# A bank for each token tile in the values' sums, zeros between the low halves of the probabilities, and two raw places for the output weights

## What is computed

```
h = layernorm(x);  q = h @ wq (32 heads of 128);  k, v = ctx @ wk, ctx @ wv (8 heads of 128, each for 4 heads of q)
q, k = rope(q), rope(k)
attn = softmax(q k^T / sqrt(128) + mask);  o = attn v;  x1 = x + tanh(g_xattn) * (o @ wo)
h1 = layernorm(x1);  logits = h1 @ route_w^T;  e = argmax(logits)
out = x1 + tanh(g_ffn) * (logits[e] * (h1 @ A[e]^T) @ Bw[e]^T)
```

## Time and profile before

| | us |
|---|---|
| median of 3 runs (lowest, highest) | 1171.74 (1171.24, 1173.85) |
| profiled execution | 1174.4 |
| its span, first to last instruction | 1172.3 |
| PE busy | 1125.3 (96%) |
| DVE busy | 927.2 (79%) |
| ACT busy | 632.2 (54%) |
| POOL busy | 564.2 (48%) |
| idle of PE ahead of line 846, for DVE line 1118 | 15.9 |

### The profile page before, as it was taken

The page is one execution under the profiler, slowest core; times in us unless marked ns, Lnnn a source line. Parts: engine busy times, 40 slices in busy tenths (PEclk is TensorE's granted clock), DMA queues, the critical chain, the costliest instruction groups (busy, mean ns, idle before and its releaser), DMA issues.

```text
span 1172.3 us, 17228 instructions
## 1 busy us (share of the span) xinstructions
PE 1125.3 (96%) x5792; PEld 922.9 (79%) x5792; DVE 927.2 (79%) x1413; ACT 632.2 (54%) x1090; POOL 564.2 (48%) x512
## 2 busy tenths in 40 slices
PE   7999999799999999999999999999999999999997
PEld 6788887677777777777778777888888888888775
DVE  7984747888778778787888888788888877788877
ACT  6452355556666666666665444555555555555441
POOL 4651467676666666666653323233333333333320
PEclk9999999899999999999999999999999999999999
DMA  6869963494545454535368625542435342431101
GB/s 225 281 226 371 301 221 129 142 365 140 190 135 189 135 189 135 189 135 190 117 224 339 191 97 157 160 163 90 168 112 188 112 166 91 162 125 65 64 1 72
DMA packets 88902, 197.89 MB, mean 169 GB/s; under 512 B 8304, under 2 KB 41200, under 8 KB 82928
## 3 DMA queue, kind: packets, MB, share of 16 engines
q1 hardware_dynamic: 88816, 196.79, 48.8%
HBM read 113.92 MB, written 82.84 MB: 168 GB/s over the span
## 4 chain that ended last, share of the span: by engine, by line
PE 49%; POOL 17%; DVE 14%; issue 13%; ACT 4%; DMA 1%; DVEq 0%; SPq 0%; POOLq 0%; ACTq 0%
PE attn L846 18%; PE proj L784 12%; POOL rot L1575 6%; PE attn L736 4%; PE score L801 4%; POOL wq_s L1550 3%; PE turned L736 2%; PE score L736 2%; DVE q_r L1033 2%; DVE o_s L1118 2%; DVE p_low L1111 2%; DVE acc L1130 2%; PE turned L812 2%; ACT p_high L1395 1%; PE attn L828 1%
## 5 line engine op out<-in xcount | busy, mean ns | idle before, releaser
L846 PE MATMUL attn<-wo_s,o_s 128*128 128x512 f32 x1536 | 386.3, 401 | 15.9 <-DVE o_s L1118 15.9
L846 PEld LDWEIGHTS attn<-wo_s,o_s 128*128 128x128 f32 x1536 | 282.1, 189 | 87.7 <-DVE o_s L1118 31.6
L784 PE MATMUL proj<-xB,wq_s 128*128 128x512 f32 x1344 | 343.7, 399 | 5.2 <-DVE q_r L1075 5.2
L1575 POOL TENSOR_TENSOR rot<-rot,tab 128x512 f32<-128x512 f32 x160 | 216.6, 1355 | 230.5 <-ACT rot L1358 230.4
L784 PEld LDWEIGHTS proj<-xB,wq_s 128*128 128x128 f32 x1344 | 248.5, 189 | 65.9 <-DVE q_r L1075 6.0
L1038 DVE TENSOR_TENSOR q_r<-q_r,rot 128x512 f32<-128x512 f32 x128 | 126.4, 988 | 44.8 <-POOL rot L1575 33.7
L1403 ACT ACTIVATE o_s<-attn 128x512 fp32r<-128x512 f32 x128 | 69.5, 596 | 147.0 <-PE attn L832 146.8
L1033 DVE TENSOR_TENSOR q_r<-q_r,tab 128x512 f32<-128x512 f32 x128 | 139.8, 1092 | 1.7 <-ACT rot L1358 1.5
L1130 DVE SCALAR_TENSOR_TENSOR acc<-attn,gates_t,acc 128x512 f32<-128x512 f32 x128 | 96.1, 751 | 54.1 <-PE attn L846 52.1
L801 PEld LDWEIGHTS score<-k_r,q_r 128*128 128x128 f32 x1024 | 124.8, 193 | 7.3 <-issue 2.6
L801 PE MATMUL score<-k_r,q_r 128*128 128x64 f32 x1024 | 122.4, 273 | 0.2 <-DVE prob_even L1095 0.2
(11 more groups left out here) (175 smaller groups left out, 1463.5 us busy)
## 6 DMA issues: line engine op xcount, KB each, us to landing
wq_kept<-wq_s SPq DMA_DIRECT2D x16, 1792.0 KB, 6.6
wq_s<-wq_kept SPq DMA_DIRECT2D x16, 1792.0 KB, 8.4
v_kept<-vst SPq DMA_DIRECT2D x64, 256.0 KB, 4.9
v_s<-v_kept SPq DMA_DIRECT2D x128, 128.0 KB, 5.0
wo_kept<-wo_s SPq DMA_DIRECT2D x32, 512.0 KB, 2.9
wo_s<-wo_kept SPq DMA_DIRECT2D x32, 512.0 KB, 5.3
k_kept<-kst SPq DMA_DIRECT2D x32, 256.0 KB, 2.1
wq_raw<-in_wq SPq DMA_DIRECT2D x16, 512.0 KB, 8.1
```

What stands on the lines that cost most here:

```text
L784: last = e.matmul(dst[:, :], wq_s[:, b % 2, A, s, kt, :], xB[:, B, mv, kt, :], start=(first and kt == 0 and m == 0), stop=(kt == 1 and m = ...
L846: last = e.matmul(attn[bp][:, :], o_s[:, s, bp, h, :], wo_s[n % WO_SLOTS][:, m, :], start=(h == 0 and i == 0), stop=(h == GROUP - 1 and i ...
L1575: e.tensor_tensor(r3, r3, sin, ALU.mult).then_inc(times_sin, 1)
```

## The change

Each bank now takes one token tile: its two twins side by side, 256 columns each. Per token tile there are two high matmuls (one for each twin) and one low matmul of 128 rows and 512 columns. For that `p_low` becomes [128, 2 tiles, 2 twins, 256], in which the rows that are not the twin's are zero; a memset on GpSimd at job 54 writes the zeros once, and `prob_low` only writes the twins' own rows. The stationary side needs high values of both twins in their own rows: `v_both`, a fifth transfer of 256 KB per unit of two steps. `attn_high`, `attn_low`, `project_out` and the waits of `times_values` go by token tile: `project_out(k, 0)` waits for the first low half alone.

The bigger `p_low` takes the place of `expert_s`, which moves onto the raw query weights; x gets places of its own (`x_near`, `x_third`); the ring of raw output weights has two tiles instead of four. So the third and fourth of them are fetched at jobs 59 and 61, and the first four are split at jobs 57, 58, 60 and 62.

```diff
@@ -43,7 +43,7 @@
 
-RAW = 4
+RAW = 2
 WO_SLOTS = GROUP + 2
@@ -84,7 +84,7 @@
     SPLITS_BESIDE[33 + _kt] = [("ctx", 3, _kt)]
-    SPLITS_BESIDE[57 + _kt] = [("wo", _kt)]
+    SPLITS_BESIDE[(57, 58, 60, 62)[_kt]] = [("wo", _kt)]
 FIRST += [w for n in sorted(SPLITS_BESIDE) for w in SPLITS_BESIDE[n] if w[0] != "wo"]
@@ -182,6 +182,7 @@
 SCORES_AFTER = 62
+ZEROS_BESIDE = 54
 ROPE_BESIDE = {51: (0, 0), 54: (0, 1), 55: (0, 2), 56: (0, 3), 57: (1, 0), 60: (1, 1), 61: (1, 2)}
@@ -297,17 +298,20 @@
         o_s = sb_at(base + 77824, "o_s", [P, 2, PAIRS, GROUP, P], F32R)
-        p_low = sb_at(base + 90112, "p_low", [P, 512], F32R)
 
...
         wq_raw = sb_at(base + 122880, "wq_raw", [P, 2, KT, 2 * DH])
-        expert_s = sb_at(base + 131072, "expert_s", [P, 2, DM])
+        x_third = sb_at(base + 131072, "x_third", [P, 2, DM])
+        p_low = sb_at(base + 131072, "p_low", [P, PAIRS, 2, GROUP * SEQ], F32R)
         copies = sb_at(base + 135168, "copies", [P, 3, CHUNK])
...
         prob_odd = sb_at(base + 92160, "prob_odd", [P, 512])
         late_s = sb_at(base + 122880, "late_s", [P, 2, DM])
+        expert_s = sb_at(base + 126976, "expert_s", [P, 2, DM])
         far_raw = [sb_at(base + place, f"far_raw{i}", [P, KT, 512]) for i, place in enumerate((135168, 122880))]
@@ -316,7 +320,9 @@
 
+        x_near = sb_at(cursor[0], "x_near", [P, 2 * CHUNKS, 512])
         raw = sb("raw", [P, RAW, 512])
+        v_both = sb("v_both", [P, 2, CHUNK_TILES, DH], F32R)
         combined = sb("combined", [P, 4, 2, P])
@@ -559,7 +567,9 @@
                 if u >= 2:
-                    e.wait_ge(values_used, SUBS * (u - 1))
+                    e.wait_ge(values_used, PAIRS * SUBS * (u - 1))
+                else:
+                    e.wait_ge(x_turned, 4 * len(X_PAIRS))
                 if u == 0 or u == 1 or G == KV_HEADS:
@@ -568,6 +578,7 @@
                                     v_kept[index, g, part, TWIN_ROWS[twin]]).then_inc(v_in[u % 2], 16)
+                e.dma_start(v_both[:, u % 2, :, :].bitcast(F32), v_kept[index, g, 0]).then_inc(v_in[u % 2], 16)
 
@@ -611,7 +622,7 @@
                 fetch_first(w)
-            ring = RAW
+            ring = KT
             for n, job in enumerate(JOBS):
@@ -647,6 +658,8 @@
                     fetch_keys(1)
+                if n in (59, 61):
+                    fetch_raw(RAW + (n - 59) // 2)
                 if n == 60:
@@ -816,26 +829,23 @@
                 tiles = [s * PAIRS + bp for bp in range(PAIRS)]
-                e.wait_ge(v_in[u % 2], 64 * (u // 2 + 1))
+                e.wait_ge(v_in[u % 2], 80 * (u // 2 + 1))
                 e.wait_ge(probs_low, 2 * k + 2)
...
                 cols = [slice(bp * GROUP * SEQ, (bp + 1) * GROUP * SEQ) for bp in range(PAIRS)]
-                for twin in range(2):
+                for bp in range(PAIRS):
                     if k:
-                        e.wait_ge(x1_added, 2 * k - 1 + twin)
-                    for bp in range(PAIRS):
-                        e.matmul(attn[twin][:, cols[bp]], v_s[:, u % 2, twin, tiles[bp], :], p_high[:, twin, cols[bp]],
-                                 start=(bp == 0), stop=False, skip_group_check=True)
-                for bp in range(PAIRS):
-                    for twin, rows in enumerate(TWIN_ROWS):
-                        last = e.matmul(attn[twin][:, cols[bp]], v_s[rows, u % 2, twin, tiles[bp], :], p_low[rows, cols[bp]],
-                                        start=False, stop=True, skip_group_check=True)
-                last.then_inc(values_used, 1)
+                        e.wait_ge(x1_added, 2 * k - 1 + bp)
+                    for twin in range(2):
+                        e.matmul(attn[bp][:, cols[twin]], v_s[:, u % 2, twin, tiles[bp], :], p_high[:, twin, cols[bp]],
+                                 start=(twin == 0), stop=False, skip_group_check=True)
+                    e.matmul(attn[bp][:, :], v_both[:, u % 2, tiles[bp], :], p_low[:, bp].rearrange("p t n -> p (t n)"),
+                             start=False, stop=True, skip_group_check=True).then_inc(values_used, 1)
 
...
                 G = k // (CHUNKS * SUBS)
-                e.wait_ge(out_low, 2 * k + 2)
+                e.wait_ge(out_low, 2 * k + bp + 1)
                 for h in range(GROUP):
@@ -1107,14 +1117,17 @@
                     if k:
-                        e.wait_ge(values_used, k)
-                    e.tensor_tensor(p_low[rows, :], turned[rows, :], p_high[rows, twin, :].bitcast(F32),
+                        e.wait_ge(values_used, PAIRS * k)
+                    else:
+                        e.wait_ge(zeros_set, 1)
+                    e.tensor_tensor(p_low[rows, :, twin, :], turned[rows, :].rearrange("p (b n) -> p b n", b=PAIRS),
+                                    p_high[rows, twin, :].bitcast(F32).rearrange("p (b n) -> p b n", b=PAIRS),
                                     ALU.subtract).then_inc(probs_low, 1)
 
-            def attn_low(k, twin):
-                src = attn[twin][:, :].rearrange("p (b h q) -> p b h q", b=PAIRS, h=GROUP)
-                high, low = (o_s[:, part, :, :, SEQ * twin:SEQ * twin + SEQ] for part in (0, 1))
-                e.wait_ge(out_high, 2 * k + twin + 1)
+            def attn_low(k, bp):
+                src = attn[bp][:, :].rearrange("p (t h q) -> p h t q", t=2, h=GROUP)
+                high, low = (o_s[:, part, bp, :, :].rearrange("p h (t q) -> p h t q", t=2) for part in (0, 1))
+                e.wait_ge(out_high, 2 * k + bp + 1)
                 e.tensor_tensor(low, src, high.bitcast(F32), ALU.subtract).then_inc(out_low, 1)
@@ -1389,18 +1402,18 @@
                 if k:
-                    e.wait_ge(values_used, k)
+                    e.wait_ge(values_used, PAIRS * k)
                 for twin, rows in enumerate(TWIN_ROWS):
...
 
-            def attn_high(k, twin):
-                if twin == 0:
-                    e.wait_ge(values_used, k + 1)
-                    if k:
-                        e.wait_ge(out_projected, GROUP * 2 * k)
-                src = attn[twin][:, :].rearrange("p (b h q) -> p b h q", b=PAIRS, h=GROUP)
-                e.activation(o_s[:, 0, :, :, SEQ * twin:SEQ * twin + SEQ], src, ACT.Copy).then_inc(out_high, 1)
+            def attn_high(k, bp):
+                e.wait_ge(values_used, PAIRS * k + bp + 1)
+                if k:
+                    e.wait_ge(out_projected, GROUP * (2 * k - 1 + bp))
+                src = attn[bp][:, :].rearrange("p (t h q) -> p h t q", t=2, h=GROUP)
+                high = o_s[:, 0, bp, :, :].rearrange("p h (t q) -> p h t q", t=2)
+                e.activation(high, src, ACT.Copy).then_inc(out_high, 1)
 
@@ -1606,6 +1619,9 @@
                     combine_weights(COMBINED_BESIDE[n])
+                if n == ZEROS_BESIDE:
+                    e.wait_ge(x_turned, 4 * len(X_PAIRS))
+                    e.memset(p_low[:, :, :, :].bitcast(F32), 0.0).then_inc(zeros_set, 1)
                 for w in WQ_BESIDE.get(n, ()):
```

More of the change, by code:

```diff
@@ L378, in build @@
         weighted, out_ready = sem("weighted"), sem("out_ready")
+        zeros_set = sem("zeros_set")
         power_set, ln_rstd, times_sin, less_max = sem("power_set"), sem("ln_rstd"), sem("times_sin"), sem("less_max")
@@ L394, in x_place @@
             turn = x_number(w) % X_PLACES
-            return expert_s[:, w[3], :] if turn == X_PLACES - 1 else raw[:, CHUNKS * turn + w[3], :]
+            return x_third[:, w[3], :] if turn == X_PLACES - 1 else x_near[:, CHUNKS * turn + w[3], :]
         def x_number(w):
```

## The result

| | before | after |
|---|---|---|
| median of 4 runs each, us | 1171.61 | 1165.51 |
| lowest, highest | 1171.24, 1173.85 | 1163.71, 1167.51 |
| profiled execution, span | 1172.3 | 1165.7 |

The ratio is 0.9944, 95% interval 0.9923 to 0.9966; on another chip 0.9933 (0.9921 to 0.9945). The forecast was 1164.2 us. That it came so near is in part luck, as the stage times show: the forecast was 1.9 us too cautious on the start, the experts and the second stretch together, and 2.8 us too hopeful on the first stretch and the end. The stages are cut at the first score matmul of a step; the last two columns are taken from one profiled execution each.

What follows compares the result with a forecast made beforehand. The loop over DVE, POOL and ACT bounds the first stretch, a gapless PE the second. Terms 2.2 + 0.8 - 2 - 0.5 - 6.1 - 1.9 = -7.5 take 1171.74 to 1164.2 us; range 1157 to 1171.

Steps and rivals of the forecast that it cites:

- Sums on PE: Values' sums and the next product on PE: 0.17 us saved per step, bounds 0.30 gained to 0.03 lost.
- the surplus of 0.19: Four high matmuls cost 0.65 = 4 x 0.114 + 0.19; half laid to waiting for 64 rows, giving 0.55.
- Zeros cost columns: Rival: pairs of 64 rows work side by side, so wide matmuls add 0.23 us a step: 1176.0 us, chance 0.06.
- The projection's wait: Second stretch: projection starts on the first low half alone; no stall, but 0.13 us goes every second step.
- First stretch: 262 to 600 us, loop over DVE, POOL and ACT: 6 rounds x 0.3 = -2 us (0 to -13).
- the steps of 374 us: First-stretch steps where DVE waits 1.18 us for POOL's chain, without PE in it: 0 gained.
- DVE gains at most its wait of 0.38, about 0.3: First-stretch steps like that of 393 us, where DVE waits for PE; every second one is held by POOL again.
- Start: Late third output weight +2.2 us (+1.8 to +4.4) and the fourth's moved subtraction +0.8 (0 to +1.2).
- Experts: Four steps from 666 to 748 us, waiting for DVE's norms: -0.5 us (0 to -2).
- End: Last four steps, PE's waits shortened: 0.3 + 0.3 + 0.64 + 0.6, -1.9 us (-1 to -2.5).
- the fourth term, 0.6 at the last step: Last step: DVE's norms and PE's second projection hang on the second low half, moved up by ACT's earlier copy.
- the clock at the end: Rival: a shorter wait keeps PE at 2.4 GHz near 1109.92, half of 6.8 us back: 1160.8 us, chance 0.19.

Runs made afterwards that it cites:

- pad_twin_banks: Kernel after, but each twin keeps its bank, low part is four matmuls of 128 rows x 256, projection waits for both halves: 1173.53 us, ratio 0.9998.
- wait_both: Kernel after, but each output projection waits for both low halves again: 1172.82 us, ratio 0.9987.
- the first pair of kernels: GpSimd's combining of query weights moved behind the first rope product, in the kernel after (1173.86 us, ratio 1.0002) and the kernel before (1180.48 us, 1.0057).
- the second pair: GpSimd's combining behind all rope products, ScalarE's odd splits in the odd step: kernel after 1182.81 us (1.008), kernel before 1191.92 us (1.0161).
- three experiments: GpSimd's combining behind the first rope product (ratio 1.0002); with a subtraction moved too and the start mended (1.0018); behind all products (1.008).
- start_alone: Kernel before with only the change's start: two raw places, later fetches and splits of the third and fourth output weight: 1177.2 us, ratio 1.0028.
- pool_late: Kernel after, GpSimd combining weights behind all rope products, ScalarE splitting odd pieces in the odd step ahead of the exponential: 1182.81 us, ratio 1.008.
- before_pool_late: Kernel before with GpSimd combining weights behind all rope products and ScalarE's odd splits moved into the odd step: 1191.92 us, ratio 1.0161.
- the moved subtraction: Kernel after, third and fourth output weight fetched one job earlier, VectorE's subtraction of the fourth behind its first row sums: 1161.9 us, ratio 0.9901.
- the earlier fetch: Kernel after with the third and fourth output weight fetched one job earlier, at jobs 58 and 60: 1163.28 us, ratio 0.991.
- pool_order: Kernel after with GpSimd's sums and differences of query weights moved behind the first rope product in even steps: 1173.86 us, ratio 1.0002.
- pool_late_fetch: pool_late with the third and fourth output weight fetched one job earlier and the fourth's subtraction behind the first row sums: 1181.27 us, ratio 1.0058.

## Why the prediction was right, step by step

**Sums on PE: right.** 0.17 us per step was forecast; sums and product behind them save 0.05 + 0.12 = 0.17 by the rows above. Its split holds too: 0.07 and 0.13 were counted ahead of the rounding down to 0.17. So does the step behind the 0.07: half of the surplus of 0.19 was put to the last high matmul's wait for the change to 64 rows, and the high matmuls went from 0.65 to the forecast 0.55; the low ones cost 0.48 for 0.46. `pad_twin_banks`, with the banks as before, has sums of 1.03 and a product of 2.75 behind them (start to start, where nothing waits), so the gain comes with the padding and not with the banks. "Zeros cost columns" is out: a padded matmul takes 0.24 us to the next start, about what wide ones do (0.23), and the sums are no longer than with four of 64 rows. This agrees with the rule on draining in the Trainium skill's "TensorEngine Tiling (Array Packing)", Key Properties, and not with a gain from tiles that work at the same time. In the kernel before, the narrow ones do start in pairs (two within 15 ns), but the four took 0.43 us where their columns alone, side by side, come to 0.23, an estimate from the 0.114 us of a wide matmul's half.

**The projection's wait: right sign, a third of the size.** "No stall, but the 0.13 goes every second step" was true of the kernel before. It failed as a price of the edit, since it was worked out at the old pace. Once PE is 0.17 a step faster, DVE's second half is 0.20 late, and taking that wait away is worth 0.36 per two steps (the 0.20 and the exposed load, 3.02 - 2.88 = 0.14); the 0.34 of the sums and the 0.13 were added as if each stood alone. The sum of both, 0.47, came near the measured 0.54, because the forecast rightly checked what would be late next (DVE's first half) for the two together.

**First stretch: too much.** The mechanism named for the steps of 374 us (DVE waits for POOL all the same) holds for all of them. The step that failed is "DVE gains at most its wait of 0.38, about 0.3": it went (12.0 to 3.5 us in all), and the wait for POOL grew by nearly the same amount (24.1 to 31.4). That PE's wait is slack there is shown by `wait_both`. That the stretch follows POOL's order, in both kernels alike, and not PE's saving is shown by the first pair of kernels; the second pair shows an order in which PE's saving does count. That moving POOL's work away from the rope products would shorten it, which I believed in three experiments, is refuted for the three orders tried.

**Start: +1.98 from job 59 on, for +3.0.** That sum has three parts, and none is the one forecast. DVE's product for job 60 comes 1.1 us late instead of 2.2. From there to the scores of step 1 another 2.3 us are lost, where 0.8 were put down for the fourth subtraction. And from step 1 to step 3 the kernel takes 30.47 us instead of 31.86, a gain of 1.4 that the forecast didn't have; the second execution on another chip has 30.39, and `wait_both` and `pad_twin_banks` have 30.95 and 30.74, so most of it comes with the padding.

The load was mis-sized: it took 2.66 us to its use, where 3.0 was the least and 3.35 were taken; and it was sent at 209.88, not at 210.35. For the 256 KB the formula of the Trainium skill's "DMA: Bandwidth & Descriptors" (one DMA's anatomy), 2.6 us, agrees with 2.66; but the page gives it for DMAs sent by GpSimd, and these are sent by SyncE. Nor does it hold for this load in general: with one store in flight, as here, the same load took 2.64 us to landing here, 3.20 in the kernel before (sent at 329.70) and 2.85 in `start_alone`. Why this one was the quickest isn't known. The fourth subtraction cost more than its 0.83 (1.78 beside a POOL product), and what it is worth is not settled apart from the 1.3 us above. The kernel after has one stretch of 3.4 us at half clock less here than before, but that gave little: its second execution has all of the kernel before's and takes 61.34 us from job 59 to step 3 instead of 61.27.

**Experts: -0.86 for -0.5**, within bounds; with both halves required (`wait_both`) 0.73 of it is gone (136.62 us). **End: -1.45 for -1.9.** PE's three waits there, of the kernel after (before 1.22, 0.61 and 1.43, the first and last in the earlier trace rows):

```profile
1102.95 0.50 PE L841 MATMUL attn<-p_high,v_s 128*128 128x256 f32 x2 [0.99 <-DVE acc L1143]
...
1115.84 0.51 PE L841 MATMUL attn<-p_high,v_s 128*128 128x256 f32 x2 [0.38 <-DVE acc L1143]
1129.52 3.04 PE L856 MATMUL attn<-wo_s,o_s 128*128 128x512 f32 x12 [0.85 <-DVE o_s L1131]
```

They fell by 0.23, 0.23 and 0.58 (0.3, 0.3 and 0.64 forecast). For the fourth term, 0.6 at the last step, at most 0.41 of the 1.45 are left. The half clock stayed for its two stretches; of the kernel after:

```profile
1104.42:1107.83 3.41, 3.41 (x18) 3.41 (x18) 1.32 (x3) 0.00 (x0) 0.00 (x0) 0.50 0.02 5
1107.83:1111.24 3.41, 3.41 (x10) 2.64 (x9) 2.17 (x4) 3.00 (x5) 1.04 (x1) 0.50 0.00 0
```

So "the clock at the end" is out too. `pool_late` and `before_pool_late` have one such stretch at the end, and their ends take 87.42 and 88.94 us instead of 89.08 and 90.53: one costs 1.6 us, and whether it comes doesn't hang on the change.

## What to carry to other kernels

Price a removed wait at the pace that the rest of the change sets, not at the old one: here 0.13 became 0.36, and without it half of the other saving was spent waiting. In a stretch set by a loop over other engines, look whom the helped engine's waits go to; a saving there is a wait renamed. When a ring of buffers is cut, send its first late load one job earlier and see what else the new order frees: with the moved subtraction this made 0.9944 into 0.9901, of which the start accounts for 3.4 us in the profiled executions.

## Not expected of the hardware

Stretches at half the granted clock come and go with small shifts of the work. One near 667 us is there in the profiled executions of the kernels before, after and `wait_both`, and absent in those with the earlier fetch, but also in `pool_order` and `pool_late`, which have the late one: it isn't the fetch that decides. Steps 27 to 35 of the kernel after take 135.89 us with it, and of the same code 134.4 without. The timed runs fit that: the four of the kernel after span 1161.9 and 1163.1 us at a mean granted clock of 0.994, and 1164.3 and 1165.7 at 0.993. In `pool_late_fetch` PE idled 1.85 us up to 275.51 and 2.32 up to 306.53, and each time a stretch at half clock followed (busy and clock, columns as in the earlier trace rows; PE full, 0.50):

```profile
272.30:275.70 3.40, 1.55 (x9) 0.98 (x8) 2.25 (x5) 1.35 (x3) 2.71 (x3) 1.00 0.68 231
275.70:279.10 3.40, 3.40 (x11) 2.81 (x11) 2.16 (x3) 3.03 (x6) 2.79 (x2) 0.50 0.00 0
279.10:282.50 3.40, 3.40 (x20) 2.88 (x19) 3.34 (x5) 1.14 (x2) 1.52 (x2) 1.00 0.79 333
```

In it PE did 11 matmuls where the next 3.4 us hold 20. In `pool_late` a pause of 1.84 up to 279.72 left the clock at full speed. Why pauses of the same length do so at some times and not at others isn't settled.
